# A GRU with expert-choice routing on one core: the tie search in two halves, its second half between the output sums, and bias loads cut into short runs

## The chip, the cores and the metric

One core of a Trainium2 chip runs one program. The metric is the device time of one execution in microseconds, given as the median of several runs. Six engines or queues matter here: TensorE (PE, with its weight loads PEld), VectorE (DVE), ScalarE (ACT), GpSimd (POOL, for masks at the start), SyncE (SP, which issues DMAs) and the 16 DMA engines behind the two queues of SP and ACT.

## The reference

For 16 sequences of 256 steps with 512 features:

```
h = cond                                     # 16 x 512
for t in range(256):                         # a GRU cell
    gi = x[:, t] @ W_ih + b_ih ; gh = h @ W_hh + b_hh
    r, z = sigmoid(gi_r + gh_r), sigmoid(gi_z + gh_z)
    n = tanh(gi_n + r * gh_n)
    h = (1 - z) * n + z * h ; hs[:, t] = h
S = softmax(hs @ router_w + router_b)        # 4096 tokens x 16 experts
G, idx = top_k(S.T, 256)                     # each expert takes 256 tokens
y[idx] += G * (hs[idx] @ expert_w + expert_b)
out = x + y                                  # 16 x 256 x 512
```

All experts share one weight matrix, so the output of a token is x plus the expert product of its state times the sum of the scores of the experts that took it. The kernel therefore computes the product for every token, and beside it the weight of each token: its scores at or above each expert's threshold, where of equal scores (ties) the first tokens fill the places that are left.

## The kernel before, in words

The 4096 tokens lie in 32 tiles (NT) of 128 tokens: 16 sequences x 8 steps. The states of all tiles stay in SBUF (`tok`, `tile(n)`).

**Start.** SP loads the first x tile, W_ih and W_hh in four quarters each (L374 to L380). ACT's queue loads the biases and cond (L475 to L478): b_ih in two pieces, b_hh in one, all three into partition 0 of tiles that are not used yet (`bih`, `bhh`, L168), and then cond. TensorE turns x and cond (L993, L998), sums the biases into a bank with rank-1 products (L1003 to L1010), projects the first inputs (L1012 to L1021) and starts step 0, for each quarter of W_hh as it lands (L830 to L835).

**The loop.** 256 steps of recurrent products (L819) on TensorE, gates on ACT and DVE; input projections, router products and the expert products of the first 12 tiles fill TensorE's time between them. The change doesn't touch it.

**The end.** After the last step, DVE and ACT search each expert's threshold in 15 rounds of counting; between rounds TensorE works on the expert products of tiles 12 to 30. Their work is counted in units: one unit is one quarter of the columns for one block of 128 rows, 16 to a tile; `expert(n)` (L922) does the next n units, up to four at once with `widest=4`. TensorE runs its program in order, so how many units stand before each wait is written out by hand: `BEYOND_UNITS[1]` are those before and after the last count (L1088, L1089), `TIE_UNITS` those before the first and the third weight product (L1099). By the count in the code 192 units are done when TensorE waits for R; tile n (from 16 on) is complete at unit 56 + 16 (n - 15).

**Ties.** DVE marks the tokens that equal the threshold (`tie`, L1506), sums them along the sequence (`prefix`, L1507), takes the number in each group of 8 tokens (`R`, L1508) and TensorE sums R over the groups before (L1094). `side` (ACT, L721) says whether a score is above, at or below the threshold, and `rank` (L1511) = prefix - 8192 x side. `need` (L1513) is the number of places left, `fit` (L1522) the limit for each group. Then for each of four quarters of the tokens (`QUARTERS` = 2, 3, 0, 1: quarter g holds tiles 8g to 8g + 7) `compare` (L1530) marks rank <= fit and `choose` (L1536) multiplies with the scores; TensorE turns the chosen scores of a quarter into weights of its tokens (L1102), and `take_weights` (L1544) copies the weights of two quarters into SBUF.

**Output.** `add_x(i)` (L1566) computes weight x product + x for the tile at place i of `OUT_ORDER`. Tiles 21 to 30 are read from PSUM, in six banks used in turn (`ffn_ring`); tiles 0 to 20 from SBUF. Tiles 12 to 15 need a `merge` (L1554) first. ACT presets the bank of tile n + 6 once the sum of tile n is out (L729). Outputs leave through SP's queue at even places (L422) and ACT's at odd ones (L733). Tile 31 is done in two halves (L949, L1586), stored by ACT (L736) and SP (L425).

DVE's order before, from `fit` on: compare 2, 3; choose 2, 3; compare 0, 1; weights of quarters 2 and 3; add_x(0); choose 0, 1; add_x(1); weights of quarters 0 and 1; add_x(2) to add_x(30); the two halves of tile 31.

Of the kernel before, what the change touches and what calls it, by code (L numbers as in the profile page):

```python
# [5 lines left out]
def gru_expert_choice_kernel(nc, x, cond, w_ih, w_hh, b_ih, b_hh, router_w, router_b, expert_w, expert_b, out):  # L6
# [80 lines left out]
    BEYOND_UNITS, TIE_UNITS = [[7, 5], [8, 2]], [6, 6]  # L87
# [5 lines left out]
    stored_tiles, psum_tiles = iter(range(IN_PSUM)), iter(range(IN_PSUM, NT))  # L93
# [18 lines left out]
    with ctx:  # L112
# [55 lines left out]
        bih, bhh = (tok[0:1, PAD + n * D:PAD + (n + G) * D].rearrange("p (g c) -> p g c", g=G) for n in (NT - 8, NT - 12))  # L168
# [305 lines left out]
        def _(act):  # L474
            act.dma_start(bih[:, 0, :], b_ih.rearrange("(o g c) -> o g c", o=1, g=G)[:, 2]).then_inc(b_loaded, 16)  # L475
            act.dma_start(bih[:, 1:, :], b_ih.rearrange("(o g c) -> o g c", o=1, g=G)[:, 0:2]).then_inc(b_loaded, 16)
            act.dma_start(bhh, b_hh.rearrange("(o g c) -> o g c", o=1, g=G)).then_inc(b_loaded, 16)
# [261 lines left out]
        def _(pe):  # L739
# [263 lines left out]
            for a in range(2):  # L1003
                for b, first in ((bih, IN), (bhh, R_)):
                    for j in range(J):
                        mm = nc.tensor.matmul(gates[0][a][Q * j:Q * (j + 1), first:first + G * HC]
                                              .rearrange("b (g k c) -> b g k c", g=G, k=KH), ones,
                                              b[:, :, a * HC * J:(a + 1) * HC * J].rearrange("p g (k j c) -> p j g k c", j=J, c=Q)[:, j],
# [100 lines left out]
        def _(dve):  # L1109
# [398 lines left out]
            V.tensor_tensor(R, prefix_ends, prefix_starts, ALU.subtract).then_inc(R_ready, 1)  # L1508

            dve.wait_ge(side_ready, 1)  # L1510
            mark(V.scalar_tensor_tensor(rank, side, -FAR, prefix, ALU.mult, ALU.add))  # L1511
            dve.wait_ge(cnt_all, ALL_ROUNDS + 2)
            need_set = mark(V.tensor_scalar(need[:, :], cnt_beyond_ps[1], -0.5, need_base[:, :], ALU.mult, ALU.add))  # L1513
# [10 lines left out]
            fits = prefix.rearrange(BY_TOKEN, b=B, g=NG)  # L1524
            ranks = rank.rearrange(BY_TOKEN, b=B, g=NG)
# [48 lines left out]
            compare(QUARTERS[2])  # L1574
            compare(QUARTERS[3])
            take_weights(slice(0, 2))
            add_x(0)
            choose(QUARTERS[2])
            choose(QUARTERS[3])
            add_x(1)  # L1580
            take_weights(slice(2, 4))
            for i in range(2, NT - 1):
                add_x(i)
            for half, cols in enumerate(HALVES):
                dve.wait_ge(last_done, half + 1)
                V.scalar_tensor_tensor(xs_tile(NT - 1)[:, cols], bank(NT - 1 + half)[:, cols], weight[:, NG - 1, NI - 1:NI],  # L1586
                                       xs_tile(NT - 1)[:, cols], ALU.mult, ALU.add).then_inc(out_ready, 1)
# [23 lines left out]
```

## Time and profile before

| | us |
|---|---|
| median of 3 runs (1095.88 to 1097.18) | 1097.17 |
| the profiled execution's own time | 1096.32 |
| its span in the profile | 1094.6 |
| PE busy (share of the span) | 1081.6 (99%) |
| DVE busy | 857.2 (78%) |
| ACT busy | 411.3 (38%) |

The span is what the profile covers; the execution's own time has 1.7 us around it. In the rows below, a timeline row has start and duration in us, engine, line, operation, destination <- sources, their shapes and the count of instructions; the bracket at its end is the time that the engine was idle before it, and what released it. Every fp32 matmul counts as two instructions, and busy times of matmuls contain the end of the pipeline, so two rows can overlap by some 0.2 us. A window row has the stretch and its length, then busy time of PE, PEld, DVE, ACT and POOL, the granted TensorE clock, the mean busy share of the 16 DMA engines and the GB/s moved. A queue row has packets, MB and the share of the 16 engines' time in the stretch. "q1" is SP's queue, "q10" ACT's. Landing is the time from the issue of a DMA to its last byte.

### The profile page before, as it was taken

What the parts mean: (1) busy time and instruction counts of PE and PEld (TensorE: products, weight loads), DVE (VectorE), ACT (ScalarE), POOL (GpSimd) and SP (SyncE); (2) the same over time, 40 slices, a digit from 0 to 9 for tenths busy, and PEclk for the clock granted to TensorE, in tenths of its full rate; (3) what the DMA queues carried; (4) which work ended last, traced back from release to release, by engine and by line L of the source; (5) the groups of instructions that cost most, each with busy time, mean ns of one, the idle gap of its engine ahead of it and who ended that gap; (6) DMA issues with size and microseconds to landing.
All of it is one profiled execution on the core that took longest, in us unless ns stands there. A gap on an engine that the chain in (4) does not pass through costs nothing.

```text
span 1094.6 us, 60966 instructions
## 1 busy us (share of the span) xinstructions
PE 1081.6 (99%) x26752; PEld 892.5 (82%) x26752; DVE 857.2 (78%) x4601; ACT 411.3 (38%) x1658; POOL 15.5 (1%) x42
## 2 busy tenths in 40 slices
PE   7999999999999999999999999999999999999998
PEld 5788888888888888888888888888888888888852
DVE  5788777877777877787777778778788777777897
ACT  1333333434333434333333333333333333333561
POOL 5000000000000000000000000000000000000000
PEclk9999999999999999999999999999999999999999
DMA  7311000000000000000000000000000000000369
GB/s 255 90 22 23 13 13 13 6 11 13 13 13 13 14 13 6 11 13 13 14 13 14 13 5 12 13 13 13 13 13 12 6 12 14 3 3 4 100 175 308
DMA packets 80448, 36.78 MB, mean 34 GB/s; under 512 B 70052, under 2 KB 70308, under 8 KB 80183
## 3 DMA queue, kind: packets, MB, share of 16 engines
q1 hardware_dynamic: 77840, 28.79, 10.8%
q8 instruction: 209, 3.42, 1.3%
q10 hardware_dynamic: 2342, 4.11, 1.2%
q14 instruction: 57, 0.46, 0.1%
HBM read 24.49 MB, written 8.39 MB: 30 GB/s over the span
## 4 chain that ended last, share of the span: by engine, by line
PE 96%; DVE 1%; DMA 1%; SPq 0%; ACT 0%; issue 0%; DVEq 0%
PE gates L819 60%; PE gates L756 26%; PE ffn_ps L883 3%; PE gates L937 3%; DMA whh<-in_L_cond_W_hh 1%; PE gates L915 1%; PE ffn_ps L937 1%; PE log_ps L972 1%; PE gates L949 0%; DVE wih L1417 0%; SPq L376 0%; PE ffn_ps L915 0%; DVE u L1186 0%; SPq L379 0%; DVE wih L1507 0%
## 5 line engine op out<-in xcount | busy, mean ns | idle before, releaser
L819 PE MATMUL gates<-whh,tok 128*16 128x192 f32 x16384 | 713.9, 326 | 3.5 <-DVE tok L1211 1.9
L819 PEld LDWEIGHTS gates<-whh,tok 128*16 128x16 f32 x16384 | 562.5, 123 | 104.5 <-DVE tok L1211 3.3
L518 ACT ACTIVATE th<-gates 128x128 f32<-128x128 f32 x512 | 139.8, 273 | 341.7 <-PE gates L819 341.5
L1186 DVE SCALAR_TENSOR_TENSOR u<-th,gates 128x64 f32<-128x64 f32 x512 | 113.5, 222 | 167.0 <-ACT th L518 166.7
L523 ACT ACTIVATE n_t<-v 128x64 f32<-128x64 f32 x512 | 131.5, 257 | 277.9 <-DVE v L1190 277.9
L756 PE MATMUL gates<-wih,xS 128*32 128x192 f32 x3024 | 146.3, 326 | 0.0
L1202 DVE STREAM_TRANSPOSE nT<-n_t 128x64 f32<-128x64 f32 x512 | 123.7, 242 | 0.0
L1193 DVE STREAM_TRANSPOSE zT<-th 128x64 f32<-128x64 f32 x512 | 122.0, 238 | 0.0
L1190 DVE SCALAR_TENSOR_TENSOR v<-u,gates 128x64 f32<-128x64 f32 x512 | 113.1, 221 | 8.8
L756 PEld LDWEIGHTS gates<-wih,xS 128*32 128x32 f32 x3024 | 100.1, 110 | 21.0
L1211 DVE SCALAR_TENSOR_TENSOR tok<-new_n,z_h 128x32 f32<-128x32 f32 x512 | 110.1, 215 | 8.7
L1198 DVE SCALAR_TENSOR_TENSOR z_h<-zT,half_h 128x32 f32<-128x32 f32 x512 | 98.5, 192 | 17.6
L756 PE MATMUL gates<-wih,xT 128*32 128x192 f32 x2016 | 105.3, 326 | 0.0
L1206 DVE SCALAR_TENSOR_TENSOR new_n<-zT,nT 128x32 f32<-128x32 f32 x512 | 96.7, 189 | 8.8
L756 PEld LDWEIGHTS gates<-wih,xT 128*32 128x32 f32 x2016 | 66.8, 110 | 13.3
L1230 DVE TENSOR_SCALAR half_h<-tok 128x64 f32<-128x64 f32 x255 | 57.5, 226 | 8.7
L756 PE MATMUL gates<-w_sums,xS 128*32 128x192 f32 x1008 | 52.7, 326 | 0.0
L756 PE MATMUL gates<-w_sums,xT 128*32 128x192 f32 x1008 | 52.7, 326 | 0.0
L483 ACT ACTIVATE gates<-bias 128x256 f32<-128x256 f32 x128 | 47.9, 375 | 0.0
L937 PE MATMUL gates<-we,tok 128*32 128x128 f32 (+1 forms) x696 | 43.9, 402 | 0.2 <-ACT gates L531 0.2
L756 PEld LDWEIGHTS gates<-w_sums,xT 128*32 128x32 f32 x1008 | 33.4, 110 | 7.7
L756 PEld LDWEIGHTS gates<-w_sums,xS 128*32 128x32 f32 x1008 | 33.4, 110 | 7.6
(202 smaller groups left out, 622.2 us busy)
## 6 DMA issues: line engine op xcount, KB each, us to landing
x_in<-in_x SPq DMA_DIRECT2D x248, 32.0 KB, 2.2
out<-tok SPq DMA_DIRECT2D x15, 256.0 KB, 4.7
xs<-in_x SPq DMA_DIRECT2D x14, 256.0 KB, 3.7
out<-tok ACTq DMA_DIRECT2D x14, 256.0 KB, 4.6
wih<-in_L_cond_W_ih SPq DMA_DIRECT2D x4, 768.0 KB, 7.1
whh<-in_L_cond_W_hh SPq DMA_DIRECT2D x4, 768.0 KB, 13.7
whh<-in_x SPq DMA_DIRECT2D x12, 256.0 KB, 3.6
we<-in_L_ffn_expert_w SPq DMA_DIRECT2D x4, 256.0 KB, 2.8
```

Source lines behind the costliest of these rows:

```text
L518: nc.scalar.activation(th[a][:, :, :].rearrange("p g c -> p (g c)"), gates[t // S % PAIRS][a][:, R_:HN], ACT.Tanh, scale=0.5).then_inc(th_ ...
L523: nc.scalar.activation(n_t[a][:, :], v[a][:, :], ACT.Tanh).then_inc(n_ready[a], 1)
L756: mm = nc.tensor.matmul(ps[Q * j:Q * (j + 1), IN:HN].rearrange("b (g k c) -> b g k c", g=G, k=KH), rows(k), columns(k, j), start=False, st ...
L819: mm = nc.tensor.matmul(gates[t // S % PAIRS][a][Q * j:Q * j + rows, R_:GC].rearrange("b (g k c) -> b g k c", g=G, k=KH), columns, by_tile ...
L937: mm = nc.tensor.matmul(bank(n)[Q * j:Q * (j + 1), cols], tile(n)[:, kc * P + Q * j:kc * P + Q * (j + 1)], we[:, kc, cols], start=False, s ...
L1186: V.scalar_tensor_tensor(u[a][:, :], th[a][:, 0, :], 1.0, ps[a][:, HN:GC], ALU.add, ALU.mult).then_inc(u_ready[a], 1)
L1190: V.scalar_tensor_tensor(v[a][:, :], u[a][:, :], 0.5, ps[a][:, IN:R_], ALU.mult, ALU.add).then_inc(v_ready[a], 1)
L1193: V.transpose(zT[a][:, :, :].rearrange("p k q -> p (k q)"), th[a][:, 1, :]).then_inc(zT_ready[a], 1)
L1198: V.scalar_tensor_tensor(z_h[a][:, :, :], zT[a][:, :, rows], 1.0, half_h[:, chunks[a], :], ALU.add, ALU.mult)
L1202: V.transpose(nT[a][:, :, :].rearrange("p k q -> p (k q)"), n_t[a][:, :]).then_inc(nT_ready[a], 1)
L1206: V.scalar_tensor_tensor(new_n[a][:, :, :], zT[a][:, :, rows], 1.0, nT[a][:, :, rows], ALU.subtract, ALU.mult).then_inc(new_n_ready[a], 1)
L1211: V.scalar_tensor_tensor(by_chunk[:, chunks[a]], new_n[a][:, :, :], -0.5, z_h[a][:, :, :], ALU.mult, ALU.add).then_inc(h_ready[a], 1)
```

## The change

- **Units.** `BEYOND_UNITS[1]` goes from [8, 2] to [8, 4]: four units stand between the last count and the wait for R, not two. `TIE_UNITS` goes from [6, 6] to [6, 27]: 27 units stand between the second and the third weight product. The total is the same.
- **Order of tiles.** The tiles that lie in SBUF go out in the order 16 to 20, 0 to 15 (before 0 to 20). The places of the PSUM tiles stay.
- **Ranks.** `need` is computed ahead of the ranks; the ranks of quarters 2 and 3 ahead of `fit`, those of 0 and 1 behind the choices of 2 and 3.
- **Order of DVE.** From `fit` on: compare 2, 3; choose 2, 3; ranks of 0, 1; weights of 2 and 3; add_x(0) to add_x(4); compare 0, 1; add_x(5), add_x(6); choose 0, 1; add_x(7), add_x(8); weights of 0 and 1; add_x(9) to add_x(30); tile 31.
- **Biases.** The three loads have the same bytes, but write them as runs of 32 values (128 bytes) that stand 40 values apart: 16, 32 and 48 runs, where each load wrote one piece (2, 4 and 6 KB). The bias products read the new layout; their number and shapes stay.

```diff
--- before.py
+++ after.py
@@ -84,13 +84,13 @@
 
     LAST_UNITS, SOFTMAX_UNITS, ROUND_UNITS = [3, 6, 4, 5], 17, 10
 
-    BEYOND_UNITS, TIE_UNITS = [[7, 5], [8, 2]], [6, 6]
+    BEYOND_UNITS, TIE_UNITS = [[7, 5], [8, 4]], [6, 27]
 
     EVACUATED = 9
     IN_PSUM = IN_LOOP + EVACUATED
 
     PSUM_PLACES = [0, 1, 2, 3, 7, 12, 17, 22, 27, 30, 31]
-    stored_tiles, psum_tiles = iter(range(IN_PSUM)), iter(range(IN_PSUM, NT))
+    stored_tiles, psum_tiles = iter([*range(NT // 2, IN_PSUM), *range(NT // 2)]), iter(range(IN_PSUM, NT))
     OUT_ORDER = [next(psum_tiles if i in PSUM_PLACES else stored_tiles) for i in range(NT)]
 
     QUARTERS = [2, 3, 0, 1]
@@ -165,7 +165,10 @@
         h0_t = tile(NT - 1)[:, 0:K * B]
         ident = tile(NT - 4)[:, 0:P]
         ones = tile(NT - 4)[0:1, P:P + Q]
-        bih, bhh = (tok[0:1, PAD + n * D:PAD + (n + G) * D].rearrange("p (g c) -> p g c", g=G) for n in (NT - 8, NT - 12))
+
+        RUN, RUNS = 40, D // Q
+        bih, bhh = (tok[0:1, PAD + n * D:PAD + n * D + G * RUNS * RUN].rearrange("p (r c) -> p r c", c=RUN)[:, :, 0:Q]
+                    for n in (NT - 8, NT - 12))
         xs = sb("xs", [P, XS, D])
 
 
@@ -472,9 +475,9 @@
 
         @block.scalar
         def _(act):
-            act.dma_start(bih[:, 0, :], b_ih.rearrange("(o g c) -> o g c", o=1, g=G)[:, 2]).then_inc(b_loaded, 16)
-            act.dma_start(bih[:, 1:, :], b_ih.rearrange("(o g c) -> o g c", o=1, g=G)[:, 0:2]).then_inc(b_loaded, 16)
-            act.dma_start(bhh, b_hh.rearrange("(o g c) -> o g c", o=1, g=G)).then_inc(b_loaded, 16)
+            act.dma_start(bih[:, 0:RUNS, :], b_ih.rearrange("(o r c) -> o r c", o=1, c=Q)[:, 2 * RUNS:, :]).then_inc(b_loaded, 16)
+            act.dma_start(bih[:, RUNS:, :], b_ih.rearrange("(o r c) -> o r c", o=1, c=Q)[:, 0:2 * RUNS, :]).then_inc(b_loaded, 16)
+            act.dma_start(bhh, b_hh.rearrange("(o r c) -> o r c", o=1, c=Q)).then_inc(b_loaded, 16)
             act.dma_start(h0, cond).then_inc(h0_loaded, 16)
             act.wait_ge(start_zeroed, 1)
             nc.scalar.activation(warm[:, 1:2], warm[:, 0:1], ACT.Tanh)
@@ -1005,7 +1008,7 @@
                     for j in range(J):
                         mm = nc.tensor.matmul(gates[0][a][Q * j:Q * (j + 1), first:first + G * HC]
                                               .rearrange("b (g k c) -> b g k c", g=G, k=KH), ones,
-                                              b[:, :, a * HC * J:(a + 1) * HC * J].rearrange("p g (k j c) -> p j g k c", j=J, c=Q)[:, j],
+                                              b.rearrange("p (g a k j) c -> p a j g k c", g=G, a=2, j=J)[:, a, j],
                                               start=False, stop=(b is bhh), skip_group_check=True)
             mm.then_inc(bias_summed, 1)
             pe.wait_ge(xT_ready, K)
@@ -1506,11 +1509,20 @@
             link(V.tensor_scalar(tie.rearrange(BY_TOKEN, b=B, g=NG), S_by_token, thr[:, :], None, ALU.is_equal))
             link(V.tensor_tensor_scan(prefix, tie, zeros16[:, :], 0.0, ALU.add, ALU.add))
             V.tensor_tensor(R, prefix_ends, prefix_starts, ALU.subtract).then_inc(R_ready, 1)
-
-            dve.wait_ge(side_ready, 1)
-            mark(V.scalar_tensor_tensor(rank, side, -FAR, prefix, ALU.mult, ALU.add))
             dve.wait_ge(cnt_all, ALL_ROUNDS + 2)
             need_set = mark(V.tensor_scalar(need[:, :], cnt_beyond_ps[1], -0.5, need_base[:, :], ALU.mult, ALU.add))
+
+            fits = prefix.rearrange(BY_TOKEN, b=B, g=NG)
+            ranks = rank.rearrange(BY_TOKEN, b=B, g=NG)
+            sides = side.rearrange(BY_TOKEN, b=B, g=NG)
+
+            def rank_ties(g):
+
+                return mark(V.scalar_tensor_tensor(ranks[:, :, g:g + 2], sides[:, :, g:g + 2], -FAR, fits[:, :, g:g + 2],
+                                                   ALU.mult, ALU.add))
+
+            dve.wait_ge(side_ready, 1)
+            rank_ties(QUARTERS[0])
             for p in range(4):
                 dve.wait_ge(xs_loaded[p], 8 * 16)
             dve.wait_ge(half_taken, IN_LOOP // 2 * 4)
@@ -1521,8 +1533,6 @@
 
             link(V.tensor_tensor_scan(fit[:, :], zeros[:, :], ties_ps, need[:, 0:1], ALU.add, ALU.subtract))
 
-            fits = prefix.rearrange(BY_TOKEN, b=B, g=NG)
-            ranks = rank.rearrange(BY_TOKEN, b=B, g=NG)
             fit_by_token = fit[:, :].rearrange("p (b g) -> p b g", b=B)
             fits_set = {}
 
@@ -1571,16 +1581,20 @@
             compare(QUARTERS[1])
             choose(QUARTERS[0])
             choose(QUARTERS[1])
-            compare(QUARTERS[2])
-            compare(QUARTERS[3])
+            late_ranks = rank_ties(QUARTERS[2])
             take_weights(slice(0, 2))
-            add_x(0)
-            choose(QUARTERS[2])
-            choose(QUARTERS[3])
-            add_x(1)
-            take_weights(slice(2, 4))
-            for i in range(2, NT - 1):
+
+            for i in range(NT - 1):
                 add_x(i)
+                if i == 4:
+                    dve.wait_ge(soft, late_ranks)
+                    compare(QUARTERS[2])
+                    compare(QUARTERS[3])
+                if i == 6:
+                    choose(QUARTERS[2])
+                    choose(QUARTERS[3])
+                if i == 8:
+                    take_weights(slice(2, 4))
             for half, cols in enumerate(HALVES):
                 dve.wait_ge(last_done, half + 1)
                 V.scalar_tensor_tensor(xs_tile(NT - 1)[:, cols], bank(NT - 1 + half)[:, cols], weight[:, NG - 1, NI - 1:NI],
```

## Rows read from the trace of the kernel before

**Rows 1.** The page, part 4: the chain that ended last, by engine.
```profile
PE 96%; DVE 1%; DMA 1%; SPq 0%; ACT 0%; issue 0%; DVEq 0%
```

**Rows 2.** The chain in order of time, 0 to 30 us: start, us, what.
```profile
5.34 15.72 DMA whh<-in_L_cond_W_hh
```

**Rows 3.** The timeline, 0 to 25 us: start, us, engine, line, operation, idle before.
```profile
6.83 1.06 PE L998 MATMUL gates<-tok 16*128 16x16 f32 x8 [1.26 <-DMA tok<-in_cond]
...
7.82 1.50 PE L1006 MATMUL gates<-tok 1*32 1x192 f32 x32
...
17.18 1.51 PE L819 MATMUL gates<-whh,tok 128*16 128x192 f32 x32
...
19.25 0.84 PE L819 MATMUL gates<-whh,tok 128*16 128x192 f32 x16 [0.56 <-DMA whh<-in_L_cond_W_hh]
...
21.10 0.84 PE L819 MATMUL gates<-whh,tok 128*16 128x192 f32 x16 [1.01 <-DMA whh<-in_L_cond_W_hh]
```

**Rows 4.** DMA queues in 0:25, 11:18.4 and 21:24 us, and the landing of L478.
```profile
q10 hardware_dynamic: 38, 0.05, 0.5%
...
q1 hardware_dynamic: 557, 3.04, 100.2%
...
q1 hardware_dynamic: 1066, 0.13, 27.7%
...
DMA to landing us min/median/max: 4.7/4.7/4.7
```

**Rows 5.** The timeline, 1062 to 1067 us.
```profile
1062.47 0.68 DVE L1511 SCALAR_TENSOR_TENSOR wih<-wih 128x512 f32<-128x512 f32 x1
...
1062.61 0.22 PE L1094 MATMUL gates<-R_padded,behind 128*32 128x64 f16 x4 [0.52 <-DVE R_padded L1508]
...
1063.07 0.21 DVE L1513 TENSOR_SCALAR need<-log_ps,need_base 128x1 f32<-128x1 f32 x1
...
1063.41 0.35 DVE L1522 TENSOR_TENSOR_SCAN fit<-zeros,need,gates 128x64 f32<-128x64 f32 x1
...
1063.80 0.49 DVE L1530 TENSOR_TENSOR wih<-wih,fit 128x128 f32<-128x128 f32 x2
1064.21 0.49 DVE L1536 TENSOR_TENSOR wih<-scores_by_expert,wih 128x128 f32<-128x128 f32 x2
...
1064.55 0.45 PE L1102 MATMUL gates<-group_of,wih 128*32 128x8 f32 x16 [0.39 <-DVE wih L1536]
...
1064.83 1.48 PE L937 MATMUL gates<-we,tok 128*32 128x128 f32 x24
1065.07 0.17 DVE L1544 COPY weight<-gates 128x16 f32<-128x16 f32 x1
...
1066.28 0.45 PE L1102 MATMUL gates<-group_of,wih 128*32 128x8 f32 x16
```

**Rows 6.** A tile's 16 units on the chain; four output sums in the timeline.
```profile
1079.63 3.43 PE ffn_ps L937 x32
...
1071.17 2.73 DVE L1566 SCALAR_TENSOR_TENSOR tok<-tok,weight,xs 128x512 f32<-128x512 f32 x4
```

**Rows 7.** A stretch of the stores; landings of L422, 1066.1 and 1088.1.
```profile
1082.00:1090.00 8.00, 7.95 (x108) 3.25 (x100) 6.55 (x11) 0.00 (x0) 0.00 (x0) 1.00 1.02 349
...
DMA to landing us min/median/max: 3.2/3.2/3.2
...
DMA to landing us min/median/max: 5.0/5.0/5.0
```

**Rows 8.** The timeline of the third and the last output sum, and L425's landing.
```profile
1067.20 0.75 DVE L1566 SCALAR_TENSOR_TENSOR tok<-ffn_ps,weight,whh 128x512 f32<-128x512 f32 x1
...
1090.02 0.48 DVE L1586 SCALAR_TENSOR_TENSOR w_sums<-gates,weight,w_sums 128x256 f32<-128x256 f32 x1 [1.24 <-PE gates L949]
1090.53 0.69 SPq L425 DMA_DIRECT2D out<-w_sums  x1
...
DMA to landing us min/median/max: 3.6/3.6/3.6
```

## The prediction

> **What bounds the kernel now.** I read the page first: the chain that ended last is 96% PE, so TensorE sets the time [rows 1]. Nothing that the change touches lies in the long middle (the 256 recurrent steps); its edits are in the first 10 us and in the last 33. So I read those two stretches closely: the start in the timeline and the chain [rows 2 to 4], the end in the timeline [rows 5], then what closes the kernel: TensorE, VectorE or the output transfers [rows 6 to 8].
>
> At the start the path is a transfer. The chain runs from 5.34 to 21.06 us through the last quarter of W_hh [rows 2]. TensorE waits 1.26 us for cond, then runs the bias products at once (it waited for no bias), and later stands idle 0.56 and 1.01 us for W_hh [rows 3]. From 11 to 18.4 us the DMA engines are fully loaded [rows 4].
>
> At the end three things run nearly level. TensorE works through units (one unit is a 128-column quarter of one row block): one tile of 16 units takes 3.43 us, 0.2145 each [rows 6]. VectorE starts one output sum (add_x) per 0.66 us: four take 2.73, the last of them 0.75, so three spacings are 1.98 [rows 6]. The outputs leave at a DMA share of 1.02 and 349 GB/s from 1082 to 1090, so they are backed up: the time to landing grows from 3.2 us for the first tile to 5.0 us for the one issued at 1088 [rows 7]. The last half tile waits 1.24 us for TensorE, is issued at 1090.53 and takes 3.6 us [rows 8].
>
> **The change, part by part.**
>
> *Two more units ahead of the ties.* TensorE ends its two units and waits 0.52 us for R [rows 5]. Two more cost 2 x 0.2145 = 0.43 us, which fits into 0.52, so R's product still starts at 1062.61. Gain 0.43 us of TensorE time. If they did not fit, R's sum would be late by the excess; there is 0.09 left over.
>
> *Ties ranked by two quarters.* Before: rank over 512 elements holds VectorE from 1062.47 to 1063.07, then need, then fit at 1063.41 [rows 5]. Now need goes first (TensorE sums its count before the two units, so it is there) and rank covers 256 elements. The trace has no rank of 256; bounds are half of 0.60 (0.30) and the whole 0.60. The 128-element compares take 0.41 for two (1063.80 to 1064.21), 0.20 each [rows 5]; between that and 0.60 at 512 a straight line gives 0.33, which I take. Need starts 1062.47, rank about 1062.60, fit about 1062.97 (R's sum, 1062.61 plus 0.25, is there by then). Fit is 0.44 us earlier than 1063.41, and the first two choices as well: TensorE gets them at 1064.11 and not 1064.55. Its six tie units (1.29 us from 1062.67; R's product starts at 1062.61 and hardly holds the queue) end at 1063.96, so it idles 0.15 us. The gain, 0.44, adds to the 0.43 because the units done by then are 200, not 198: 0.87 us.
>
> *The last two quarters chosen between output sums.* Before: two compares before the weights copy, where VectorE waits for TensorE anyway; six units; then TensorE waits for the third choice until 1066.28 (units begin at 1064.83 and end at 1066.12: 0.16 idle), and the products take 0.28, until 1066.56, as those of 1064.55 to 1064.83 [rows 5]. Now 27 units follow from 1064.39 and end at 1070.18. VectorE: the late rank (0.33) sits where the compares sat, weights are copied at 1064.63 (1064.11 + 0.52, as 1064.55 to 1065.07), add_x(0) at 1064.84 (the copy's 0.17 and a start), five sums to 1068.14, compares 0.41, two sums, choice at 1069.87, and TensorE can start 0.34 later (as 1064.21 to 1064.55) at 1070.21. Idle 0.03, products to 1070.49, 227 units done. Before, 204 were done at 1066.56, and unit 227 ended at 1066.56 + 23 x 0.2145 = 1071.49. **TensorE is 1.0 us ahead**, and the last half comes at 1089.0. The cover of the moved choices is thin: every 0.1 us that VectorE is later there is 0.1 us of TensorE idle. What is queued behind TensorE's wait is everything to the end.
>
> VectorE's own sum: it starts add_x(0) 0.44 earlier (before at 1065.28, the copy plus 0.21), but the compares (0.41), once in a wait, are now in its busy stretch. From place 9 on it is only 0.03 ahead. Before, it idled 1.24 us ahead of the last half at 1090.02 [rows 8]; with 1.0 taken 0.24 is left, so VectorE does not close the kernel. The changed order (tiles 16 to 20 first, since only quarters 2 and 3 have weights) leaves every sum its length; the four merges (0.4 each) move behind, to places 24 to 28. Banks: tile 27 needs the sum at place 0, tile 24 is finished at unit 200, so before add_x(3); no wait is added. ACT and SP keep their issue counts.
>
> *The outputs.* They, not TensorE, decide what of the 1.0 us arrives. An issue follows the end of its sum by 0.03 (1090.02 + 0.48 to 1090.53). Before: from the third tile (its sum ran 0.75 from 1067.20, so issued at 1067.98) they never starve; the last lands at 1094.15 (1090.53 + 3.6) [rows 8]. With the first tile's 3.2 us, and 29 tiles' worth after it, s = (1094.15 - 1067.98 - 3.2)/29 = 0.79 us per tile. After: first issue 1064.84 + 0.78 = 1065.62, sums 0.66 apart, and through the interruptions the 0.13 per tile gained holds (five tiles gain 0.65, the compares take 0.41), so all 32 are back to back: 1065.62 + 3.2 + 31 x 0.79 = 1093.3. TensorE alone would allow 1089.5 + 2.8 (a half tile, 3.2 less 0.4) = 1092.3. **End gain 0.85 us.** Bounds: the start of the outputs alone gives 0.45, TensorE's 1.0 is the top.
>
> *Biases in short runs.* Three loads with one long packet each (2, 4, 6 KB) become 96 runs of 128 bytes. The 38 packets of that queue [rows 4] are 16 rows of cond and 3 biases, each with their semaphore writes. Price: x_in's 128-byte packets, 1066 in 27.7% of 16 engines over 3 us, 12.5 ns each [rows 4]; 96 are 1.2 us of one engine, 0.08 us of each. I take 0.0, bounds +0.1 and, if W_hh's last packets are on the biases' engine, -0.48 (below).
>
> The Trainium skill (DMA: Bandwidth & Descriptors, Specifications) says that transfers under 512 bytes are read, modified and written, which speaks against this edit. By the row they cost 12.5 ns for 128 bytes, 2.5 times W_hh's time per byte and still nothing here. Were the row's price to double by that rule, an estimate, the sum would be -0.7 and not -0.85.
>
> **Sum:** -0.85 us. The profiled execution took 1096.32 us (span 1094.6, 1.7 around it), which gives 1095.5. The three runs' median, 1097.17, lies 0.85 above that execution and their spread is 1.3. From the median it is 1096.3; I say **1095.9**, the middle.
>
> **Rivals.**
>
> *A: the start gains too.* All three biases pass through one DMA engine each time. 12 KB at 6 KB per 0.24 us (557 packets in 7.4 us on 16 engines, nearly all 6 KB, [rows 4]) are 0.48 us. If the three are on the same engine and it is the one on which W_hh lands last, the chain's first piece shortens by up to 0.48 - 0.08 = 0.4 us. For: the weights' 6.3 MB and x's 0.26 at 414 GB/s need 15.8 us, from about 2.5 to 18.4, and TensorE waits to 21.10, so some engine is late by over a microsecond [rows 3, 4]. Against: 0.48 does not explain so much; something else is on the late engine. Total -1.25: 1095.5. Chance 0.2.
> The Trainium skill (same page, Why a DMA increments its semaphore by 16 and not by 1) has a load on as many engines as divide its slowest dimension, on the lowest-numbered ones; by that rule the three biases share one engine. The packet count agrees with one each; which engine, no row shows.
>
> *B: the outputs give nothing back.* If they are bound by rate from the first tile, only the earlier start counts, and a thin VectorE lead starves them later: -0.4, 1096.3. Chance 0.2.
>
> *C (slower): cond comes late.* cond is issued behind the biases on ACT's queue. Each engine now has six short packets before cond's; where each waits for two 6 KB packets of the other queue (0.24 us each), cond is 2.9 us later. TensorE's idle time before W_hh is 0.56 + 1.01 = 1.57 [rows 3], so the end is 1.3 us later, less 0.85: +0.5, 1097.6 on the median. It decides from 1.57 us of delay on, and turns the sign from 2.4. Against: cond's 4.7 us to landing [rows 4] against 3.2 for an unhindered tile [rows 7] is 1.5 for all that it waits now. Chance 0.07.
>
> *D: the late choices miss.* VectorE later than 1070.2 by d costs TensorE d, but the outputs hide the first 1.0 of it; nothing is lost unless d is over 1. Inside the forecast.
>
> The forecast itself has 0.53.
>
> **Numbers.** A measurement of this kernel tells about 0.2% (2.2 us) from no change. None of the cases reaches 2.2 us below 1097.17; only A with a spread of a microsecond does. Chances: faster by over 0.2% 0.10, within 0.2% 0.85, slower 0.05. The range reaches from A less 0.8 of spread (1094.7) to C (1097.6).
>
> **What would show it.** TensorE's idle before R's product under 0.15 us; fit about 0.4 us earlier and L1102's first product near 1064.1; its third near 1070.2 with under 0.1 idle; DMA share over 0.9 from the first microsecond of output; the last half's sum near 1089.0 with its transfer taking over 3.6 us, since it is backed up more. W_hh's wait near 21.1 (20.7 would be A; cond's wait over 2.5 us would be C). It is wrong if the last sum comes no earlier, or if the last transfer takes 2.8 us, so that TensorE decides.

## Result: slower by 2.8 us, and the profile after

The changed kernel took 1098.94 us (median of 11 runs, 1097.56 to 1100.09); the kernel before, on the same chip, 1096.16 (11 runs, 1095.05 to 1097.18). The ratio is 1.0024, with a 95% interval of [1.0017, 1.0032], so 2.6 us (1.9 to 3.5). This ratio, here and below, is the recorded one and not the quotient of the two medians; where the two differ, the interval decides. I had said 1095.9, within 1094.7 to 1097.6, and gave "slower by over 0.2%" a chance of 0.05: the sign, the size and the range were wrong.

The profiled execution of after took 1098.12 us with a span of 1096.4, against 1096.32 and 1094.6 before: 1.8 us of the 2.8. It was the second fastest of the eleven, so the profile shows less of the loss than the median. First the page, by engine: the chain is still TensorE, and a row of its second part is new, cond's transfer.

```profile
PE 97%; DVE 1%; DMA 1%; ACT 0%; issue 0%; ACTq 0%; DVEq 0%
...
PE gates L822 61%; PE gates L759 26%; PE ffn_ps L886 3%; PE gates L940 3%; PE gates L918 1%; PE ffn_ps L940 1%; PE gates L750 1%; PE log_ps L975 1%; DMA tok<-in_cond 1%; PE gates L952 0%; DVE wih L1420 0%; PE gates L1009 0%; PE ffn_ps L918 0%; DVE u L1189 0%; DVE wih L1510 0%
```

Lines of the code stand 3 lower after the new layout (L998 is L1001, L1006 is L1009, L747 is L750, L819 is L822) and up to 14 lower at the end. Now the start: the chain in order of time, 0 to 30 us (start, us, what), in the place of [rows 2].

```profile
0.80 0.65 ACTq L478
...
1.48 0.60 ACTq L479
...
2.12 0.61 ACTq L480
...
2.76 6.53 DMA tok<-in_cond
...
13.81 7.18 PE gates L750 x128
...
25.26 2.86 PE gates L822 x64
```

Before, the chain ran from 5.34 to 21.06 us through the last quarter of W_hh. Now it runs through the issues of the three bias loads, then 6.53 us of cond's transfer, then TensorE, with one pause of 0.96 us while ACT copies the summed biases (L632). TensorE's timeline of the same stretch, against [rows 3]:

```profile
9.33 1.06 PE L1001 MATMUL gates<-tok 16*128 16x16 f32 x8 [3.41 <-DMA tok<-in_cond]
10.32 2.52 PE L1009 MATMUL gates<-tok 1*32 1x192 f32 x32
13.81 7.18 PE L750 MATMUL gates<-wih,xT 128*32 128x192 f32 x128 [0.96 <-ACT bias L632]
20.80 2.79 PE L822 MATMUL gates<-whh,tok 128*16 128x192 f32 x64
```

The wait for cond is 3.41 us and not 1.26, so cond's product starts 2.50 later (9.33 for 6.83). The same bias products take 2.52 us and not 1.50. The 64 products with W_hh run in one piece: the two waits for W_hh are gone because TensorE comes to each quarter later than the transfer does (the last quarter lands at 21.4). The second step of the recurrence starts at 25.26, before at 23.62. These 1.64 us stay until the end (R's product starts at 1064.22, before at 1062.61).

The four landings of ACT's queue, in order of issue (L478, L479, L480, and L481 for cond):

```profile
DMA to landing us min/median/max: 1.9/1.9/1.9
...
DMA to landing us min/median/max: 3.4/3.4/3.4
...
DMA to landing us min/median/max: 4.8/4.8/4.8
...
DMA to landing us min/median/max: 6.5/6.5/6.5
```

With the issues at 0.80, 1.48, 2.12 and 2.76 they land at 2.7, 4.9, 6.9 and 9.3 us: 2.0 to 2.4 apart, though they hold 2, 4, 6 and 32 KB. In the other executions of this order of loads (experiments 1 and 4) the steps are 1.3 to 2.4 us. 768 KB of weights, one of SP's loads, take 1.9 us at the 414 GB/s of the start, so each small load comes home about one big load after the one ahead of it. The Trainium skill (DMA: Bandwidth & Descriptors, Queues, rings and completion order) has each DMA engine take turns between the queues, a whole packet from one before it goes to the other, with some 9 to 17 descriptors in a packet. What that page calls a packet holds several of what the profile counts as packets: a 768 KB load is 128 rows of 6 KB, eight for each of the 16 engines if they are spread evenly. The spacing of the landings agrees with that in size; experiment 2 below agrees only in part.

The second loss is the clock. The windows view (us, PE, PEld, DVE, ACT, POOL busy, PEclk, DMA share, GB/s), before:

```profile
8.00:11.00 3.00, 2.02 (x48) 1.41 (x44) 1.51 (x5) 1.58 (x6) 1.90 (x8) 0.95 1.02 422
11.00:14.00 3.00, 3.00 (x44) 2.55 (x40) 1.62 (x6) 0.22 (x1) 1.94 (x8) 0.50 1.03 421
14.00:18.00 4.00, 4.00 (x104) 3.69 (x99) 3.93 (x3) 0.00 (x0) 3.79 (x3) 0.99 1.00 408
```

And after:

```profile
8.00:11.00 3.00, 1.67 (x20) 1.45 (x24) 0.53 (x3) 0.00 (x0) 1.80 (x8) 0.94 1.01 406
11.00:14.00 3.00, 2.04 (x28) 1.07 (x24) 1.55 (x5) 1.07 (x4) 1.95 (x7) 0.50 1.02 420
14.00:18.00 4.00, 4.00 (x60) 2.86 (x58) 3.93 (x6) 0.73 (x3) 2.37 (x3) 0.56 1.02 418
```

A granted clock of 0.50 is the 1.2 GHz level. Before, it held from 11 to 14 and was gone from 14 to 18; after, it holds through most of that stretch too (0.56). In slices of half a microsecond the half level lasts from about 10.7 to 14.1 us before and from about 10.7 to 17.5 after. TensorE had stood idle for 3.41 us before it, where it had been 1.26; whether that is the reason is taken up in experiment 4. From 14 to 18 us TensorE is busy throughout in both, but completes 104 products before and 60 after.

The end, from R's product on (timeline of after, start, us, operation, against [rows 5] and [rows 8]):

```profile
1064.08 0.21 DVE L1513 TENSOR_SCALAR need<-log_ps,need_base 128x1 f32<-128x1 f32 x1
1064.21 0.41 DVE L1521 SCALAR_TENSOR_TENSOR wih<-wih 128x256 f32<-128x256 f32 x1
...
1064.22 0.22 PE L1097 MATMUL gates<-R_padded,behind 128*32 128x64 f16 x4
...
1064.73 0.35 DVE L1534 TENSOR_TENSOR_SCAN fit<-zeros,need,gates 128x64 f32<-128x64 f32 x1
...
1065.87 0.45 PE L1105 MATMUL gates<-group_of,wih 128*32 128x8 f32 x16
...
1071.97 0.45 PE L1105 MATMUL gates<-group_of,wih 128*32 128x8 f32 x16
...
1090.78 0.48 DVE L1600 SCALAR_TENSOR_TENSOR w_sums<-gates,weight,w_sums 128x256 f32<-128x256 f32 x1 [0.59 <-PE gates L952]
...
1091.29 0.55 SPq L428 DMA_DIRECT2D out<-w_sums  x1
```

And the landing of that last store (L428, before L425):

```profile
DMA to landing us min/median/max: 4.7/4.7/4.7
```

Less the 1.61 us that come from the start, the last half's sum is at 1089.17 (before 1090.02, forecast 1089.0): TensorE's part came. But the last store now takes 4.7 us and not 3.6, so it lands at 1094.38 on the scale of before, against 1094.13: nothing of the 0.85 is left. The load on the DMA engines does not explain this, for it falls well before the end. The windows of the last microseconds:

```profile
1092.00:1093.00 1.00, 0.00 (x0) 0.00 (x0) 0.00 (x0) 0.00 (x0) 0.00 (x0) 1.00 0.99 339
1093.00:1094.00 1.00, 0.00 (x0) 0.00 (x0) 0.00 (x0) 0.00 (x0) 0.00 (x0) 1.00 0.76 258
1094.00:1095.00 1.00, 0.00 (x0) 0.00 (x0) 0.00 (x0) 0.00 (x0) 0.00 (x0) 1.00 0.07 26
```

And the queue of the instruction fetches in the last 6 us (packets, MB, share of 16 engines):

```profile
q8 instruction: 1, 0.02, 1.0%
```

From 1094 on a share of 0.07 is left, which is about one engine of 16; the store is home at 1096.0. In the same stretch one packet of 16 KB of instructions was fetched, 1.0% of 16 engines over 6 us, so 0.96 us of one engine. In the kernel before no fetch falls in its last 6 us. After has 26776 products on its page, before 26752. From two units ahead of R's product on, ten units are now made singly where six were, and each single unit in place of a quarter of a wide one costs 6 instructions more: 24 in all.

### The profile page after: what moved, and what is told of

It reads as the page before. It is cut to its first block, busy times and chain, and to the rows that moved or that the text cites. A ratio compares the mean times of both kernels' runs of the same rounds, so it can differ in the third digit from the quotient of the medians.

```text
span 1096.4 us, 61015 instructions
## 1 busy us (share of the span) xinstructions
PE 1082.2 (99%) x26776; PEld 885.3 (81%) x26776; DVE 857.0 (78%) x4602; ACT 411.6 (38%) x1658; POOL 11.4 (1%) x42
## 3 DMA queue, kind: packets, MB, share of 16 engines
q1 hardware_dynamic: 77840, 28.79, 10.7%
## 4 chain that ended last, share of the span: by engine, by line
PE 97%; DVE 1%; DMA 1%; ACT 0%; issue 0%; ACTq 0%; DVEq 0%
PE gates L822 61%; PE gates L759 26%; PE ffn_ps L886 3%; PE gates L940 3%; PE gates L918 1%; PE ffn_ps L940 1%; PE gates L750 1%; PE log_ps L975 1%; DMA tok<-in_cond 1%; PE gates L952 0%; DVE wih L1420 0%; PE gates L1009 0%; PE ffn_ps L918 0%; DVE u L1189 0%; DVE wih L1510 0%
## 5 line engine op out<-in xcount | busy, mean ns | idle before, releaser
L822 PE MATMUL gates<-whh,tok 128*16 128x192 f32 x16384 | 713.0, 326 | 1.9 <-DVE tok L1214 1.9
L822 PEld LDWEIGHTS gates<-whh,tok 128*16 128x16 f32 x16384 | 558.4, 123 | 106.5 <-DVE tok L1214 3.3
```

What stands on the lines that cost most here:

```text
L822: mm = nc.tensor.matmul(gates[t // S % PAIRS][a][Q * j:Q * j + rows, R_:GC].rearrange("b (g k c) -> b g k c", g=G, k=KH), columns, by_tile ...
```

## Experiments

Two questions stood after this: which of the two parts loses the time, and by what. "Before" in what follows is the kernel before, in runs on the same chip; a bracket behind a ratio is its 95% interval.

**1. The two parts apart.** The first kernel is the one after with the loads, the layout and the operand of the biases as before; the second is the one after with the units, the ranks, the choices and the order of tiles and sums as before, which is the kernel before with the new biases. Of each edit, one line, against after:

```diff
...
-            act.dma_start(bih[:, 0:RUNS, :], b_ih.rearrange("(o r c) -> o r c", o=1, c=Q)[:, 2 * RUNS:, :]).then_inc(b_loaded, 16)
+            act.dma_start(bih[:, 0, :], b_ih.rearrange("(o g c) -> o g c", o=1, g=G)[:, 2]).then_inc(b_loaded, 16)
...
```

```diff
-    BEYOND_UNITS, TIE_UNITS = [[7, 5], [8, 4]], [6, 27]
+    BEYOND_UNITS, TIE_UNITS = [[7, 5], [8, 2]], [6, 6]
...
```

The end alone:

> The changed kernel with the three bias loads and their products as before; ties, units and order of tiles as changed. Theory 1 (the bias loads alone cost the time: they hold back cond, and TensorE starts late): cond is waited for until 6.8 us again, step 1 starts at 23.6 us, and the kernel is faster than the one before, by 0.3 to 0.9 us, because the last output sum comes about 0.9 us earlier; what of it reaches the end depends on the outputs. Rival 2 (the end of the changed kernel costs time too: its outputs are bound by their rate and one engine is late): within 0.3 us of the kernel before, though the last sum is 0.9 us earlier. Rival 3 (the new order at the end is slower in itself): over 0.5 us slower than before.

The biases alone:

> The kernel before with nothing changed but the three bias loads in runs of 128 bytes and the products that read them. Theory 1: cond lands at about 9.3 us, TensorE starts the projections near 13.8 and step 1 near 25.3 us (before 23.6), the whole kernel is 1.6 to 2.8 us slower. Rival (the start loses only part; the ties' change costs the rest): below 1.3 us slower.

The end alone took 1096.34 us against 1096.39 (ratio 1.0 [0.9991, 1.0009]), the biases alone 1099.0 against 1096.39 (1.0018 [1.0009, 1.0027]). By the medians the biases alone lose 2.6 us, by the ratio 2.0 (1.0 to 3.0): the loss is theirs. Of the end no gain shows, but its interval reaches 1.0 us to either side, so this run by itself does not exclude the 0.85; the traces of experiment 5 say more. The profiled execution of the biases alone was one of its quickest, 1097.37 us, and shows the pattern of after in a smaller size:

```profile
8.22 1.06 PE L1001 MATMUL gates<-tok 16*128 16x16 f32 x8 [1.50 <-DMA tok<-in_cond]
9.21 2.22 PE L1009 MATMUL gates<-tok 1*32 1x192 f32 x32
...
24.16 2.86 PE L822 MATMUL gates<-whh,tok 128*32 128x192 f32 x64 [1.02 <-DVE tok L1214]
```

Cond landed at 8.2 us here, and at 9.3 in after with the same loads: the wait differs from execution to execution, and with it the loss.

**2. Is it the number of the small loads?** To the biases alone, a fourth load is added by cutting b_hh in two, with the same bytes in the same 96 runs:

```diff
-            act.dma_start(bhh, b_hh.rearrange("(o r c) -> o r c", o=1, c=Q)).then_inc(b_loaded, 16)
+            act.dma_start(bhh[:, 0:RUNS, :], b_hh.rearrange("(o r c) -> o r c", o=1, c=Q)[:, 0:RUNS, :]).then_inc(b_loaded, 16)
+            act.dma_start(bhh[:, RUNS:, :], b_hh.rearrange("(o r c) -> o r c", o=1, c=Q)[:, RUNS:, :]).then_inc(b_loaded, 16)
...
-            pe.wait_ge(b_loaded, 3 * 16)
+            pe.wait_ge(b_loaded, 4 * 16)
```

> As the run with the bias edit alone, but b_hh is loaded by two DMAs (16 and 32 runs) in place of one (48): the same 96 runs and bytes in four DMAs. Theory A (a turn for each DMA: on every engine each DMA of ACT's queue waits while the engine serves one DMA of SP's queue, some 8 packets of 0.24 us): cond lands 1.9 to 2.6 us later again, near 11.5 us, and step 1 starts 1.5 to 2.6 us later than with three. Theory B (the number or the size of the packets delays cond): no later than the 0.6 us that one more issue takes. Nothing is said of the other DMAs.

It took 1099.63 us (1.0024 [1.0015, 1.0033]), 0.6 over the three loads, which the spread of the medians doesn't settle. The trace says more than the time:

```profile
10.30 1.89 PE L1002 MATMUL gates<-tok 16*128 16x16 f32 x8 [4.07 <-DMA tok<-in_cond]
12.12 2.78 PE L1010 MATMUL gates<-tok 1*32 1x192 f32 x32
...
27.10 1.21 PE L823 MATMUL gates<-whh,tok 128*32 128x192 f32 x24 [1.02 <-DVE tok L1215]
```

The loads landed at 2.7, 4.8, 7.2 and 10.0 us: the added one comes 2.8 us behind the one ahead of it, without a byte more. Cond, which I had expected near 11.5, came home at 10.3, 2.1 later than in the execution of the biases alone that stands above, but only 1.0 later than in after, and 0.3 behind the load ahead of it, where it had been 2.4. The direction is shown, a turn for each load only in part.

**3. Cond ahead of the short-run biases.** The biases alone again, with the same bytes and the same number of loads; only the order differs:

```diff
+            act.dma_start(h0, cond).then_inc(h0_loaded, 16)
             act.dma_start(bih[:, 0:RUNS, :], b_ih.rearrange("(o r c) -> o r c", o=1, c=Q)[:, 2 * RUNS:, :]).then_inc(b_loaded, 16)
...
-            act.dma_start(h0, cond).then_inc(h0_loaded, 16)
```

> As the run with the bias edit alone, but cond is issued ahead of the three bias loads. Theory A (a turn for each DMA): cond lands by 4 us, the last bias load near 9.3 us in cond's old place, so the bias products start near 9.3 us, a microsecond before those of the changed kernel (10.4), and step 1 starts about 1 us earlier than there (24.2). Theory B (packets of cond's own are slow behind short ones): all is loaded by 7 us and step 1 starts at 23.6 us as before.

1097.02 us, 1.0006 [0.9997, 1.0015]. Cond lands at 2.6, and the biases at about 4.5, 6.4 and 9.1, so that b_hh is now the last of four:

```profile
9.25 2.78 PE L1009 MATMUL gates<-tok 1*32 1x192 f32 x32 [2.30 <-DMA tok<-in_L_cond_b_hh]
13.00 8.09 PE L750 MATMUL gates<-wih,xT 128*32 128x192 f32 x128 [0.97 <-ACT bias L632]
...
25.36 1.88 PE L822 MATMUL gates<-whh,tok 128*32 128x192 f32 x40 [1.02 <-DVE tok L1214]
```

What waits is whatever stands last, and not cond as such. TensorE had done cond's product (1.06 us) by then, and the wait is 2.30 and not 3.41; by the medians the kernel is 2.0 us better than with cond last, by the ratios 1.3. This profiled execution was the slowest of the kernel's ten (1098.98), with the half clock from about 8 to 18.5 us; I had expected its second step at 24.2, and the clock is what I left out.

**4. The clock by itself.** The kernel after, all of its loads and waits kept, with TensorE multiplying zeros into an unused bank where it would wait for cond:

```diff
+            for _ in range(7):
+                set_bits(log_ps[:, :, :].rearrange("p g c -> p (g c)"))
```

> The changed kernel with seven rounds of products of zeros on TensorE (28 matmuls of 512 columns, about 3 us) while it waits for cond; they write zeros into a bank that holds zeros. Theory C1 (part of the loss is the clock: TensorE stands idle for cond, then works at half clock for twice as long as before): cond lands as late, near 9.3 us, but the half-clock stretch is shorter than 6.8 us or earlier, the bias products take 1.5 us and not 2.5, and step 1 starts 0.7 to 1.3 us earlier than in the changed kernel (25.3); the kernel is 1 to 2 us faster than the changed one. Rival C2 (the wait is all): the bias products and projections take as long as in the changed kernel, step 1 at 25.3.

1096.71 us, 1.0001 [0.9993, 1.001] against before; the kernel after has 1.0024. Its timeline:

```profile
9.54 1.50 PE L1011 MATMUL gates<-tok 1*32 1x192 f32 x32
12.03 5.41 PE L750 MATMUL gates<-wih,xT 128*32 128x192 f32 x128 [0.98 <-ACT bias L632]
...
21.67 0.84 PE L822 MATMUL gates<-whh,tok 128*16 128x192 f32 x16 [1.35 <-DMA whh<-in_L_cond_W_hh]
```

And its windows, against those above:

```profile
11.00:14.00 3.00, 2.02 (x53) 1.94 (x53) 1.10 (x4) 1.81 (x6) 1.84 (x8) 1.00 1.03 417
14.00:18.00 4.00, 4.00 (x107) 3.81 (x100) 3.97 (x5) 0.00 (x0) 2.32 (x3) 1.00 1.01 417
```

The clock is 1.00 where it was 0.50 and 0.56; the bias products take 1.50 us again, the projections 5.41 for 7.18, and W_hh's transfer ends the wait once more. Cond was late all the same (landed at 8.5, before at 6.8, after at 9.3). With the full clock its lateness no longer reaches the second step, which waits for W_hh.

How much is the clock's? The zeros give back 2.2 of 2.8 us (1098.94 to 1096.71). But this kernel's last instruction fetch starts 6 us before its end, 1.7 us ahead of the issue of its last store, and not within the last stores, which is worth something of its own (next experiment). So its measure is the end alone without that fetch, 1095.88: 0.8 of loss is left at the start, where the biases alone lose 2.6. By this difference of medians about two thirds are the clock's; the medians' own spread is too wide to say it closer. The trace agrees, with the second step at 24.19 (23.62 before, 25.26 after). The run takes away every stretch at half clock, that of the kernel before as well, so it says what the clock costs in all and not what the longer stretch costs.

What is left in the trace, 24.19 less 23.62, is W_hh and not cond: its last quarter ends the wait at 21.67, before at 21.10, the same 0.57. The short runs go with a late W_hh in every trace. With them its last quarter lands at 21.4 to 22.0 us (after and experiments 1 to 4, five traces), with the one-packet loads at 20.6 to 21.2 (eight traces). I priced it at nothing and no run shows why. Late loads and clock need each other: the late load uses up TensorE's slack ahead of W_hh, and only then does work at half the clock cost in full. The granted clock of the timed runs shows both sides of this. Its mean is 0.9951 in after, 0.9955 with the biases alone, 0.9966 with the end alone, 0.9975 with the zeros and 0.9967 to 0.9972 in the runs of before; but it is also 0.9958 with cond first, which loses only 0.6.

The Trainium skill (TensorE: Matmul & The Clock Gate, HAM oscillation) describes how waits for a transfer throttle the clock, so that the work behind them starts slow. Before, after and the zeros agree in the direction: 1.26 us idle and 3.4 us at half clock, 3.41 idle and 6.8, none idle and none at half clock. The other traces do not order themselves by that wait. The end with 28 (next experiment) waited 1.17 us for cond and had 0.50 from about 7.7 to 14.5 us, yet its second step starts at 23.22:

```profile
8.00:11.00 3.00, 2.79 (x33) 1.35 (x32) 1.42 (x5) 0.15 (x1) 1.80 (x8) 0.50 1.01 416
...
23.22 2.86 PE L819 MATMUL gates<-whh,tok 128*32 128x192 f32 x64 [1.03 <-DVE tok L1211]
```

With cond first (experiment 6) one execution had no wait for cond and the same 6.8 us at half clock (second step at 23.45), another none before 21 us. So that work at half clock costs when no slack is left is shown; that the longer wait for cond made the stretch longer is argued from three traces, with others against it.

**5. What ate the gain at the end?** Two readings: the outputs are bound by their rate, or the 24 added instructions brought a fetch of instructions into the last stores. The end alone again, with 28 units and not 27, a multiple of four, which restores the number of instructions:

```diff
-    BEYOND_UNITS, TIE_UNITS = [[7, 5], [8, 4]], [6, 27]
+    BEYOND_UNITS, TIE_UNITS = [[7, 5], [8, 4]], [6, 28]
```

> The changed ties with the bias loads as before, and 28 units before the late quarters in place of 27: then as many units are done four at once as in the kernel before, so TensorE runs 24 matmul instructions fewer than with 27. Theory 1 (the 0.9 us that the ties gain is given back by one DMA engine that fetches 16 KB of instructions while the last outputs leave; the longer stream of TensorE brings that fetch forward into them): no fetch in the last 4 us, the last half tile lands under 4 us after its issue (4.5 with 27), and the kernel is 0.5 to 1.0 us faster than the one before. Rival 2 (the outputs are bound by their rate alone): the last landing stays 4.5 us after its issue and the kernel is within 0.3 us of the one before.

And the reverse, the kernel before with 24 more instructions and not a column more:

```diff
-                    expert(TIE_UNITS[i // 2], widest=4)
+                    expert(TIE_UNITS[i // 2], widest=1 if i else 4)
```

> The kernel before; only four of the units ahead of the third quarter are done one at a time and not four at once: 24 matmul instructions more, the same products. Theory 1 (instruction fetch in the last outputs): the last output sum starts as late after R as before (27.7 us), a fetch falls into the last 4 us, the last half tile takes 4.3 us or more to land in place of 3.6, and the kernel is 0.3 to 1 us slower. Rival 2: no difference beyond 0.2 us anywhere.

The end with 28 took 1095.88 us against 1096.18 (0.9999 [0.999, 1.0008]), the narrow units 1097.04 (1.0008 [1.0, 1.0017]). The time alone is at the edge of what these runs tell. The traces are clear. With narrow units the last sum stands where it was before, 27.74 us behind R's (1062.50 and 1062.28), but its store takes longer:

```profile
1090.24 0.48 DVE L1586 SCALAR_TENSOR_TENSOR w_sums<-gates,weight,w_sums 128x256 f32<-128x256 f32 x1 [1.24 <-PE gates L949]
1090.75 0.54 SPq L425 DMA_DIRECT2D out<-w_sums  x1
...
DMA to landing us min/median/max: 4.1/4.1/4.1
...
q8 instruction: 1, 0.02, 1.0%
```

I had expected the fetch in the last 4 us. It starts 4 to 5 us before the end in this kernel, in after and in the end alone, so beside the last stores; before and the kernel with 28 have none in their last 6 us. The latter's last store lands 31.2 us behind R's sum (`R`, the start of that row; landing is issue plus time to landing), against 31.85 before, 32.35 with narrow units, and 32.1 and 31.9 in after and the end alone. By this pair the end saves 0.65 us.

The other traces say the same. With the old end and no fetch beside the last stores (before, the biases alone, experiments 2 and 3, before with cond first) it is 31.5 to 32.0. With the new end and no such fetch (28 units four times, and the zeros with 27) it is 30.5 to 31.3, 0.8 less in the mean. The three traces with such a fetch are the highest of their kind. So the end did save 0.65 to 0.8 us, and what came with the added instructions took it away. That the fetch itself is what delays the store is argued from its place; the number of instructions is what was varied.

**6. The end and cond's place together.** The old biases, the end with 28, and cond issued ahead of the biases (they are one packet each); and the kernel before with cond ahead alone:

```diff
+            act.dma_start(h0, cond).then_inc(h0_loaded, 16)
             act.dma_start(bih[:, 0, :], b_ih.rearrange("(o g c) -> o g c", o=1, g=G)[:, 2]).then_inc(b_loaded, 16)
...
-            act.dma_start(h0, cond).then_inc(h0_loaded, 16)
```

> As the run with 28 units, and cond issued ahead of the three long bias loads. If cond's lateness costs the kernel before nothing (it waits for W_hh at 21.1 us in any case), step 1 starts within 0.2 us of 23.6 and the time is that of the run with 28 units. Rival: TensorE starts the projections a microsecond earlier, so that less of them falls in the half-clock stretch and runs that start slow are rarer: 0.3 us or more faster.

> The kernel before with cond issued ahead of the bias loads and nothing else changed. If the 0.6 us of the run with 28 units and cond first came from the ties, this one is within 0.3 us of the kernel before; if it came from cond, it is 0.3 to 0.8 us faster.

The first took 1095.54 against 1096.18 (0.9991 [0.9982, 1.0]); before with cond ahead took 1096.06 against 1096.38 (0.9995 [0.9986, 1.0004]), no difference that shows. In the profiled execution of the first, the second step starts at 23.22, no earlier than with 28 alone, and the last half's sum at 1088.87, and the last store lands 3.3 us after its issue at 1089.38. It was run a second time, and once with the zeros (four times four products) in front of cond's product:

> The run with 28 units and cond first once more, on the chip of the two beside it: 0.3 to 1.0 us faster than the kernel before.

> The changed ties with 28 units, the long bias loads as before, cond issued first, and four rounds of products of zeros on TensorE ahead of its wait for cond. If runs of the others differ by how long TensorE works at half clock at the start, this one has no half-clock stretch before 20 us, and its time is 0.3 to 1 us under that of the run without the zeros and 1 to 1.5 us under the kernel before. Rival: the start is bound by W_hh at 20.7 to 21.1 us in any case, and the zeros change nothing (within 0.3 us).

1095.16 and 1095.63 against 1096.38 (0.9994 [0.9985, 1.0003] and 0.9995 [0.9986, 1.0004]). The zeros bring nothing that shows here, where I had hoped for 0.3 to 1 us: TensorE does not wait for cond, the clock is still at half from about 11 to 14 us, and W_hh's last quarter holds the start anyway. Both intervals of the kernel without the zeros reach 1. Its 22 runs together have a median of 1095.4, the 60 of before beside them 1096.3, and the means differ by 0.96 us (0.57 to 1.33 by resampling the runs). That is over two chips and not one comparison. On it I take this kernel to be faster than before by some 0.6 to 1 us, under 0.1%; no single comparison shows it.

## Why the prediction was wrong

**Short-run biases (failed).** The step was "I take 0.0, bounds +0.1". It priced 96 packets at 12.5 ns each, the engines' time for them, and put the wait of the loads behind them at nothing. In after's trace each small load landed 2.0 to 2.4 us behind the one ahead, and cond, fourth in line, at 9.3; with one long packet each it had come at 6.8. W_hh's last quarter came 0.3 later too, and the half clock lasted 6.8 us for 3.4. Measured for the biases alone: 2.6 us by the medians, 2.0 (1.0 to 3.0) by the ratio, where the bound said 0.1. The packets' own price, even doubled, would have moved the sum by 0.15, which is far too little. What about a run makes the load late was not separated: its shortness, or its being spread over more engines. Three loads in a few long runs, spread as widely, would tell, and were not tried.

**Rival C (held, and underrated).** It named the place (cond on ACT's queue behind the biases), a delay of 2.9 (measured 2.50 in after's trace) and the slack of 1.57 before it decides. Its price was 1.3 at the start: the profiled execution has 1.64, the comparison 2.0 to 2.6. That 1.64 came out near 1.3 is partly luck. By C's own sum the measured delay of 2.50 less the slack of 1.57 would be 0.9; the bias products at half clock added 1.02, and TensorE made up 0.3 more than the slack. What C left out is the clock: at full clock (experiment 4) the late cond cost nothing that reached the second step. Its evidence against was thin: I took the 1.5 us by which cond was slower than a free tile for all that it waits, when it had been queued behind three packets in all, and was to be queued behind 96, six for each engine.

**Rival A (no).** W_hh's last quarter came no earlier but later: 15.7 us after its issue in both traces, and the issue at 5.68 for 5.34.

**The units ahead of the ties (right).** No idle of TensorE is left ahead of R's product (0.52 before). That two more units bring four more single ones with them was not counted (below).

**The ranks (mechanism right, size off).** Fit came 0.29 earlier and not 0.44: on before's scale at 1063.12, where I had 1062.97. The rank of 256 took 0.41 where I took 0.33, and fit starts 0.52 behind its start.

**The late choices (right).** On before's scale the first product is at 1064.26 (forecast 1064.11) and the third at 1070.36 (1070.21), with no idle ahead of it. The last half's sum is 0.85 earlier (1.0 less those 0.15). VectorE still waits for TensorE there, 0.59 us.

**The outputs (failed, nearer to rival B).** Of "End gain 0.85 us" nothing shows in the comparison (1096.34 to 1096.39, 1.0 us either way); rival B had 0.4. B's cause is not it: without the fetch beside the last stores the gain in the traces is 0.65 to 0.8, so the rate from the first tile was roughly as worked out. The step that failed is a term that the sum put at nothing, without a word on it: the 24 instructions that the new numbers of units add. With them a 16 KB fetch falls beside the last stores. Added to the kernel before, they cost 0.5 us in the trace (32.35 for 31.85) and 0.9 by the medians (1097.04 to 1096.18, an interval that reaches 1.0).

**The range.** It was built on a median of three runs, 1097.17, which eleven runs put at 1096.16; on that, C would have been 1096.7. Its upper end was C's 1097.6 with nothing added for the spread of 1.3 that the three runs showed. Even with it, 1098.9, it would just have missed.

## What to carry to other kernels

While a bulk load fills the DMA engines, count the loads ahead of a critical one on its own queue, not their bytes: each of the short-run ones came about 2 us behind the one ahead of it here, where three one-packet loads let cond land at 6.8 in all. So issue first what is needed first. When a wait ahead of a stretch of products grows, look at the granted clock behind it before pricing only the wait. Work at half clock costs where the slack behind it is gone, and harmless products in the wait kept the clock up in one case here and not in the other. And count the instructions of an edit: 24 more of them went with a fetch beside the last stores and a store that landed half a microsecond later.

## What the runs showed of the hardware that I had not expected

- Three small loads of short runs and cond behind them, on one queue, landed 2.0 to 2.4 us apart beside 768 KB loads on the other (2.7, 4.9, 6.9, 9.3 us), though 96 runs of 128 bytes are 1.2 us of one engine. Other executions have steps of 1.3 to 2.8 us, and one of 0.3.
- In one execution with 28 zero products in the wait the granted clock stayed at 1.00 over the first 22 us (experiment 4), while with the sixteen of experiment 6 it was 0.50 from 11 to 14 us, as before. The half level lasted from 3.4 to 10.3 us in the traces, and differed between kernels with the same loads: in before from 10.7 to 14.1 us, in the end with 28 from about 7.7 to 14.5.
- A fetch of 16 KB took one engine 0.96 us at the end of after. And in the profiled execution of the end alone TensorE stood for 1.66 us (from 1031.23) in the middle of a row of products, with nothing that it waited for; the last fetch before it, below for 1030 to 1031 us, started before 1030.3.

```profile
1032.89 0.53 PE L937 MATMUL gates<-we,tok 128*32 128x128 f32 x11 [1.66 <-issue]
...
q8 instruction: 1, 0.02, 7.1%
```

The profiled executions of the biases alone and of experiment 3 have such stalls of 0.5 and 1.0 us at the same products, most others none. They may be a part of the spread between runs of one kernel. Whether a fetch causes them stays open: none starts within these stalls, and kernels without a stall have fetches near there as well (before, in 1032 to 1033 us).
